# Aggregation 2 of a four-layer graph network: two blocks of features at a time, with separate waits for the high and the low part

## The reference, cut to what matters

```python
def _L2_gnn_ref(x, W, b, src, dst):
    deg_out = jnp.clip(jax.ops.segment_sum(ones, src, num_segments=N), 1.0)
    deg_in = jnp.clip(jax.ops.segment_sum(ones, dst, num_segments=N), 1.0)
    h = x * (deg_out ** (-0.5))[:, None]
    agg = jax.ops.segment_sum(h[src], dst, num_segments=N)
    agg = agg * (deg_in ** (-0.5))[:, None]
    return agg @ W + b
...
x = _layernorm(x + _L1_gnn_ref(...), axis=-1)
x = _layernorm(x + _L2_gnn_ref(x, L2_gnn_W, L2_gnn_b, src, dst), axis=-1)
x = _layernorm(x + _L3_gnn_ref(...), axis=-1)
```

## Time and profile before

| | us |
|---|---|
| median of 3 runs | 599.36 |
| lowest and highest of them | 595.47, 599.69 |
| the profiled execution's own time | 599.38 |
| its span, first to last instruction | 597.7 |

### The profile page before, as it was taken

The page is one execution under the profiler, slowest core; times in us unless marked ns, Lnnn a source line. Parts: engine busy times, 40 slices in busy tenths (PEclk is TensorE's granted clock), DMA queues, the critical chain, the costliest instruction groups (busy, mean ns, idle before and its releaser), DMA issues.

```text
span 597.7 us, 7939 instructions
## 1 busy us (share of the span) xinstructions
PE 499.0 (83%) x2461; PEld 344.5 (58%) x2461; DVE 396.0 (66%) x894; ACT 251.7 (42%) x435; POOL 303.1 (51%) x328
## 2 busy tenths in 40 slices
PE   4999999999999997999993446676879777799875
PEld 2544459997899943899882001133435434365765
DVE  7999986768758868111563637555776577687475
ACT  7677741131485127211025424343434435445235
POOL 8999829210013015930003777777777777773000
PEclk9999999999999999799997577788989989799989
DMA  7900000000001200000766899999999999973004
GB/s 259 269 1 0 2 2 1 0 1 1 1 1 33 109 0 0 2 0 0 293 234 246 299 400 365 381 383 397 395 385 357 401 394 400 383 201 101 2 1 172
DMA packets 35604, 102.64 MB, mean 172 GB/s; under 512 B 6635, under 2 KB 7277, under 8 KB 35562
## 3 DMA queue, kind: packets, MB, share of 16 engines
q1 hardware_dynamic: 22150, 58.51, 26.5%
q0 software_dynamic: 13344, 43.53, 20.1%
q10 hardware_dynamic: 68, 0.09, 0.0%
HBM read 96.99 MB, written 5.12 MB: 171 GB/s over the span
## 4 chain that ended last, share of the span: by engine, by line
PE 44%; POOL 14%; DVE 14%; DMA 12%; issue 8%; ACT 5%; DVEq 2%; ACTq 0%; SPq 0%
PE ps L1200 19%; POOL xg L490 14%; DMA xg<-x_dram,srcT_i 12%; PE ps L1223 10%; DVE hot_code L815 4%; PE ps L1345 2%; PE ps L1252 2%; PE ps L1377 2%; PE ps L1366 2%; PE ps L1155 2%; ACT countsT L592 2%; DVE counts L826 2%; DVE ea L1020 1%; DVE stats L904 1%; PE ps L1177 1%
## 5 line engine op out<-in xcount | busy, mean ns | idle before, releaser
L490 POOL DMA_INDIRECT xg<-x_dram,srcT_i x168 | 172.0, 1024 | 114.7 <-DMA x_dram<-xn 63.8
L1345 PE MATMUL ps<-ea,hot_w 128*32 128x512 f32 x336 | 99.8, 735 | 65.7 <-ACT ea L657 65.5
L1020 DVE TENSOR_TENSOR ea<-ea,xg 128x512 f32<-128x512 f32 x168 | 108.9, 690 | 35.5 <-DMA xg<-x_dram,srcT_i 35.2
L657 ACT ACTIVATE ea<-ea 128x2048 f32<-128x2048 f32 x41 | 78.3, 1910 | 116.7 <-DVE ea L1020 116.7
L1345 PEld LDWEIGHTS ps<-ea,hot_w 128*32 128x32 f32 x336 | 18.1, 123 | 125.5 <-ACT ea L657 72.2
L426 POOL TENSOR_SCALAR hot_lo<-iota_n,src_loT 128x128 bf16<-128x128 f16 x105 | 66.3, 648 | 3.2 <-PE ps L1155 2.3
L1035 DVE TENSOR_TENSOR x3T<-x3T,ps 128x128 f32 x84 | 24.3, 289 | 45.4 <-issue 27.7
L815 DVE TENSOR_SCALAR hot_code<-iota_c,codeT 128x380 bf16<-128x380 f16 x168 | 49.8, 356 | 1.7 <-issue 0.8
L1200 PE MATMUL ps<-counts,xs_hi 128*128 x120 | 45.4, 379 | 3.9 <-POOL xs_lo L450 3.9
L1200 PE MATMUL ps<-counts,xs_lo 128*128 x120 | 44.3, 369 | 0.0
L1177 PE MATMUL ps<-w_s,xT 128*128 128x512 f32 (+1 forms) x80 | 40.8, 591 | 0.0
(11 more groups left out here) (180 smaller groups left out, 946.6 us busy)
## 6 DMA issues: line engine op xcount, KB each, us to landing
ea<-in_edge_attr_dram SPq DMA_DIRECT2D x41, 1024.0 KB, 9.7
w_s<-in_L_gnn_W_dram SPq DMA_DIRECT2D x5, 1024.0 KB, 8.8
xg<-x_dram,srcT_i POOLq DMA_INDIRECT x168, 7.5
xn<-in_x_dram SPq DMA_DIRECT2D x3, 768.0 KB, 8.8
x_dram<-xn SPq DMA_DIRECT2D x9, 256.0 KB
out_dram<-xn SPq DMA_DIRECT2D x9, 256.0 KB
w_s<-in_L_gnn_W_dram SPq DMA_DIRECT2D x2, 512.0 KB, 12.2
b_b<-in_L_gnn_b_dram SPq DMA_DIRECT2D x3, 256.0 KB, 10.3
```

The lines of the kernel that those rows point to most:

```text
L490: pool.indirect_dma_start(out=xg[0:n, slot, r, :], out_offset=None, in_=x3_dram[:, :], in_offset=bass.IndirectOffsetOnAxis(ap=srcT_i[0:n, ...
L657: act.activation(ea[s][:, :, :], ea[s][:, :, :], ACT.Relu).then_inc(relu_done, 1)
L1020: dve.tensor_tensor(ea[s][0:n, r, :], ea[s][0:n, r, :], xg[0:n, slot, r, :], ALU.add).then_inc(add_done, 1)
L1345: ins = pe.matmul(ps[at_w:at_w + EW, 4 + g // 2 % 2, :], hot_w[:, g % RING, 2 * b + r, :], ea[g % RING][:, 2 * b + r, :], start=(r == 0), ...
```

## The change

For layer 2 alone, the blocks of features are taken in pairs, (0, 1) and then (2, 3). `two_blocks` goes through the node tiles; at each tile it issues the two high matmuls (one for each block, each into its own bank) and then the two low ones. Aggregations 0 and 1 keep their order. The wait for a tile is now in two: for `xs_done` before the high matmuls and for `xs_ready` before the low ones, and only in the pair that has block 0. The wait for `agg_evac[2]` comes once for each pair, for the later block of the two.

```diff
+                def two_blocks(parts, rhs, ccs, n):
+
+                    for j in range(NT):
+                        for part, part_ready in zip(parts, (xs_done, xs_ready)):
+                            if 0 in ccs:
+                                pe.wait_ge(part_ready, j + 1)
+                            for cc in ccs:
+                                ins = pe.matmul(ps[:, cc, 0:CH], part[0:rows(j), j, P * cc:P * cc + P], rhs[0:rows(j), j, n],
+                                                start=(j == 0 and part is parts[0]), stop=(j == NT - 1 and part is parts[1]))
+                                if j == NT - 1 and part is parts[1]:
+                                    ins.then_inc(agg_done[layer], 1)
+
                 def chunks(parts, rhs):
                     with pe.Fori(0, NCH) as i:
                         n = bass.ds(i * CS, CH)
-                        for cc in range(blocks):
+                        if layer == 2:
+                            for ccs in ((0, 1), (2, 3)):
+                                pe.wait_ge(agg_evac[layer], i * blocks + ccs[1] + 1)
+                                two_blocks(parts, rhs, ccs, n)
+                        for cc in range(0 if layer == 2 else blocks):
                             pe.wait_ge(agg_evac[layer], i * blocks + cc + 1)
                             products(parts if layer else parts[0:1], rhs, cc, n, True, layer > 0)
```

## The result

The changed kernel takes **592.74 us**, median of 21 runs (589.42 to 597.11), against 599.12 us for the kernel before in as many (595.47 to 601.01). The ratio is 0.9905, with a 95% interval from 0.9887 to 0.9922, so it is faster by 0.8 to 1.1%. The forecast was 593.0.

A forecast was written before the change was run, and what follows sets the result against it. TensorE's own rate on 222 matmuls behind POOL's last xs_lo was taken to bound the changed loop. Gains of 3.4 + 0.4 + 2.6 = 6.4 us from 599.38 gave 593.0 us, range 589.8 to 597.0.

The forecast's parts named there:

- Price of a matmul: Aggregation loop at full clock: 0.1906 us for each matmul, waits already met taken at nothing.
- the slower case: Changing the bank at every matmul costs time behind the last wait; up to 625 us, chance 5%.
- Step 1: First chunk: block 1 moves ahead of the last low-part wait, leaving 204 matmuls instead of 222; 3.4 us.
- Step 2: Tenth tile of the first chunk: the split wait lets two high matmuls run before the last low part; 0.4 us.
- Step 3: TensorE's clock around the last waits stays full instead of falling to the lower level; 2.6 us, lower bound 0.
- the first rival: TensorE's clock falls all the same, leaving 3.8 us of gain; 595.6 us, chance 22%.
- Step 4: ACT and DVE drain both banks of a pair one behind the other without a stall; nothing booked.
- Step 5: After the loop, edge loads, projection, layer norm, store and gathers move by the same time; the whole tail shifts.
- Sum: Whole kernel: 3.4 + 0.4 + 2.6 = 6.4 us gained, giving 593.0 us.
- faster by over 1%: Whole kernel: a gain beyond the 1%, 6.0 us, that a measurement tells from no change; chance 0.48.
- The rivals: Clock falls, 595.6 us, 22%; gain swallowed in the gather stage, 599.4, 8%; bank changes slow it, 625, 5%.

The follow-up runs named there:

- the pairs alone: Changed kernel with one wait again: all four matmuls of a tile wait for the low part; 592.37 us against 597.99 for the kernel before, ratio 0.9903.
- The matmuls into the spare bank: Kernel before plus two unread matmuls into bank 7 after each of nine first-chunk tiles of block 0; 595.87 us against 597.99, ratio 0.9961.
- the split alone: Kernel before, block by block, with only the wait split into xs_done and xs_ready; 599.55 us against 599.14, ratio 1.0007.

## Why the prediction was right

*Price of a matmul.* 0.1906 us was used. In the changed kernel the last two chunks go from 250.72 to 281.28, 30.56 / 160 = 0.1910:

```profile
250.72 0.54 PE L1212 MATMUL ps<-counts,xs_hi 128*128 x2
...
281.28 1.09 PE L1239 MATMUL ps<-w_hi,z_hi 128*128 128x512 f32 x4
```

Changing the bank at every matmul thus costs at most 0.4 ns, and the slower case had no ground. With three blocks side by side the same 160 matmuls take 30.50 us (247.66 to 278.16), as in the kernel before. The waits that are met at once, doubled in number, are in that same figure.

*Step 1, 3.4 us.* Shown by the pairs alone: 204 matmuls in 39.20 us by the chain at full clock, where 222 with the clock kept up took 42.78. That is 3.6 us for 18, of which some 0.2 go with the branch in the second of them; 18 x 0.1906 = 3.4 stands. TensorE kept up, by a smaller margin than forecast: the backlog took 4.9 us for 24 matmuls (232.67 to 237.61) instead of 4.6, again because of the slow first one.

*Step 2, 0.4 us.* Shown by the same kernel against the changed one: 39.20 - 38.84 = 0.36.

*Step 3, 2.6 us.* Right in kind and about right in size. The matmuls into the spare bank give 2.3 us in the chain and a ratio that means 2.3 us (1.1 to 3.6) in the time. That the clock would stay was judged from stretches that looked alike, not from a rule, and the stretch came out busier than forecast: in the 7 us before the last release TensorE was busy for 5.64 us instead of 4.9, and the longest idle time was 0.62 us instead of about 1. The forecast also took the one execution of before as the rule. In the split alone the clock fell 3.3 us ahead of the last release instead of 4.7, and cost 1.7 us. So the term differs between kernels. Whether it differs between executions of one kernel is not shown: both executions of the split alone had the fall in the same place, and the kernel before was seen once.

The section "A second HAM failure mode: psum-queue depth-cycling" of the Trainium skill's "TensorE: Matmul & The Clock Gate", weighed under the first rival, tells of a clock that swings in a kernel that cycles through PSUM banks with short idle times between its groups. The trace of the changed kernel does not show that: it changes the bank at each matmul, has idle times of up to 0.62 us between its bursts, and its granted clock stayed at 1.00 in all three executions seen.

*Step 4, nothing.* Right. ACT reads both banks of a pair in one go, and DVE is through at 252.56, while the banks are wanted again at about 258.4:

```profile
250.81 0.92 ACT L641 CAST z_hi<-ps 128x418 f32 x2 [6.71 <-PE ps L1212]
...
251.47 1.09 DVE L971 TENSOR_TENSOR z_lo<-ps,z_hi 128x418 f32 x2 [6.52 <-ACT z_hi L641]
```

*Step 5.* Right: the tail moved as a whole, also for the version with three blocks.

*Sum.* 6.4 us was forecast for the stretch, 6.2 were seen in the profiled execution, and the medians of 21 runs lie 6.4 apart. The ratio itself, 0.9905, means 5.7 us, and its interval, 4.7 to 6.8 us, holds all three. That the median came within 0.3 us of the forecast is in part luck: the interval is 2.1 us wide, and the clock's term rests on one execution. The chance of "faster by over 1%" was near even since the gain lay on that bound; it came out at 0.95%, just within. The rivals fell: the clock stayed, the tail followed, the bank change costs next to nothing. One reading of the forecast is off without effect: the three runs of before lie 4.2 us apart, not 4.3.

## What to carry to other kernels

Where an engine waits for inputs piece by piece and then does the rest at full rate, count what stands behind the last release: widen the first pass (more accumulations side by side, one PSUM bank each) until the waits are filled, and the kernel is bound by the engine alone; here three blocks side by side fitted and were 2.4 us better than two. Such a pass can have a second yield on TensorE: here the clock fell while matmuls came one or two at a time between waits, and the dense stretch behind them began at the low clock, which cost 1.7 to 2.6 us. The two yields were separated by matmuls whose result nobody reads. Splitting a wait by operand is worth the few matmuls that it releases at the last piece, and here no more.

## What the runs showed of the hardware

The clock fell without a long standstill. In the kernel before it fell at about 236.7 us, just after TensorE had begun again behind 1.88 us of idle time. In the split alone it fell at 239.2 us, in a stretch of single matmuls with no idle time above 0.81 us between them. It stayed at 1.00 in the pairs alone, across an idle time of 1.12 us, with four matmuls between the waits. So the length of the longest idle time alone does not sort these cases; the runs do not show what does.

The chips differ. The kernel before took 654 us on one chip and 598 to 599 on others. It has no trace on the slow chip, but four of its variants have. Their first gathers come at the times of the other chips, for the pairs alone at 317.99 us on both, and all of the difference lies behind them, in the stage of gathers and edge loads. There the 202 us from 318 us on moved 318 to 328 GB/s in these four executions, against 376 to 382 in the nine executions on other chips.
